# Experts' rows turned in blocks by the vector engine instead of by TensorE

## The reference, cut to what matters

```python
xn = _rmsnorm(x_flat, norm_weight, EPS)               # x * rsqrt(mean(x*x)+eps) * norm_weight
gate_vals, expert_idx = jax.lax.top_k(probs, TOP_K)
dispatch = jnp.zeros((E, CAP, Hd), x.dtype).at[e_flat, slot].add(contrib)
dm = dispatch[MLP_START:]                             # 12 experts x 1024 slots x 128 channels
h = jnp.einsum('ech,efh->ecf', dm, fc1_weight) + fc1_bias[:, None, :]
h = jax.nn.gelu(h, approximate=False)                 # 512 hidden units
out_mlp = jnp.einsum('ecf,ehf->ech', h, fc2_weight) + fc2_bias[:, None, :]
```

## Time and profile before

| | |
|---|---|
| median of 3 runs | 927.08 us |
| profiled execution | 927.48 us, of which its span is 925.7 us |
| TensorE (PE) busy | 829.0 us, 90% |
| VectorE (DVE) busy | 724.6 us, 78% |
| ScalarE (ACT) busy | 723.1 us, 78% |
| GpSimd (POOL) busy | 601.4 us, 65% |
| mean granted TensorE clock | 0.98 |

### The profile page before, as it was taken

How to read it: one execution, slowest core, us unless ns; L and a number is a source line. 1 busy time by engine, 2 the same in 40 slices (tenths; PEclk the granted TensorE clock), 3 DMA queues, 4 the chain that set the end, 5 groups by cost and what they waited for, 6 DMA issues and landing times. The chain is left out here.

```text
span 925.7 us, 20647 instructions
## 1 busy us (share of the span) xinstructions
PE 829.0 (90%) x7499; PEld 316.7 (34%) x7500; DVE 724.6 (78%) x932; ACT 723.1 (78%) x1323; POOL 601.4 (65%) x610
## 2 busy tenths in 40 slices
PE   0687269999999999999999999999999999999996
PEld 0454112222222225676867632222222222222222
DVE  5798899999999993101011089999999999999996
ACT  0578899998999897444353569899998999899996
POOL 3355247777777663999999226757567575766772
PEclk9999669999999999999999999999999999999999
DMA  8833111111111112333242211102111111210202
GB/s 221 302 68 76 32 28 33 49 40 51 51 26 40 29 45 79 112 102 121 91 142 71 94 46 22 39 20 60 37 23 45 44 36 30 70 31 17 68 17 55
DMA packets 71229, 59.39 MB, mean 64 GB/s; under 512 B 33770, under 2 KB 58178, under 8 KB 71136
## 3 DMA queue, kind: packets, MB, share of 16 engines
q1 hardware_dynamic: 61520, 48.06, 18.2%
q0 software_dynamic: 8192, 9.37, 3.9%
q10 hardware_dynamic: 1424, 0.76, 0.4%
HBM read 31.58 MB, written 30.02 MB: 67 GB/s over the span
## 5 line engine op out<-in xcount | busy, mean ns | idle before, releaser
L733 ACT ACTIVATE pr<-ps 128x512 f32<-128x512 f32 x1024 | 555.2, 595 | 57.6 <-PE ps L853 25.0
L1154 DVE TENSOR_SCALAR ps<-ps 128x1024 f32<-128x1024 f32 (+1 forms) x585 | 588.5, 1084 | 10.9 <-PE ps L843 10.9
L873 PE MATMUL ps<-pr,vp 128*32 128x256 f32 x4096 | 320.7, 391 | 3.1 <-ACT pr L733 0.2
L853 PE MATMUL ps<-q,kz 64*128 64x512 bf16 x1024 | 200.5, 389 | 25.3 <-DVE ps L1154 20.6
L843 PE MATMUL ps<-q,kz 62*128 62x512 bf16 x1024 | 196.2, 381 | 2.3 <-DMA q<-parts_dram 1.4
L519 POOL DMA_INDIRECT xs<-eout,idxs x128 | 129.0, 1008 | 95.7 <-ACT pr L733 75.7
L873 PEld LDWEIGHTS ps<-pr,vp 128*32 128x32 f32 x4096 | 86.5, 108 | 210.4 <-ACT pr L733 186.4
L504 POOL DMA_INDIRECT disp<-xn,idx x128 | 125.8, 983 | 45.8 <-ACT pr L733 26.1
L853 PEld LDWEIGHTS ps<-q,kz 64*128 64x128 bf16 x1024 | 49.0, 93 | 254.0 <-DVE ps L1154 246.3
L1174 DVE TENSOR_TENSOR pr<-ps,parts 128x1024 f32<-128x1024 f32 x12 | 14.7, 1224 | 150.8 <-PE ps L941 150.8
L759 ACT ACTIVATE pr<-ps,b1s 128x512 f32<-128x512 f32 x96 | 65.8, 687 | 53.7 <-PE ps L930 53.7
(11 more groups left out here) (122 smaller groups left out, 531.0 us busy)
## 6 DMA issues: line engine op xcount, KB each, us to landing
moved<-att SPq DMA_DIRECT2D x480, 8.0 KB
disp<-pr SPq DMA_DIRECT2D x12, 512.0 KB, 4.8
eout<-pr SPq DMA_DIRECT2D x12, 512.0 KB, 2.9
y<-in_x SPq DMA_DIRECT2D x8, 512.0 KB, 7.8
out<-y SPq DMA_DIRECT2D x7, 512.0 KB, 3.5
w<-in_w1t SPq DMA_DIRECT2D x12, 256.0 KB, 3.1
w<-in_w2t SPq DMA_DIRECT2D x12, 256.0 KB, 3.3
xs<-disp SPq DMA_DIRECT2D x6, 512.0 KB, 4.9
```

The costliest lines, as they stand in the source:

```text
L733: act.activation(pr[:, c % BUFS, 2 * pair + k, :], ps[:, score_bank(i, k), :], ACT.Exp, scale=SLOPE).then_inc(S["exps"], 1)
L853: last = pe.matmul(ps[:, score_bank(i, k), :], kz[r:r + TILE, hg, pair, kc * P:(kc + 1) * P], q2[r:r + TILE, hg, qh * HALF:(qh + 1) * HALF ...
L873: last = pe.matmul(acc[32 * g:32 * g + 32, cols], vp[:, hg, kc, g, :], pr[:, c % BUFS, g % PAIRS * 2 + g // PAIRS, cols], start=(kc == 0 a ...
L1154: last = dve.tensor_scalar(s, s, 0.0, 1.0 / SLOPE - 1.0, ALU.max, ALU.mult)
```

## The change

The loading of `dd[u]` is split into four transfers, one for each group of 32 channels. In the transfer for channels 32r to 32r+31, partition 32r + t takes, from slots t, 32 + t, 64 + t and so on, 32 channels (128 bytes) each. VectorE then turns all 32x32 blocks of the 128x1024 tile with one instruction, straight from `dd[u]` to `dt_`. TensorE's transposes and ScalarE's copies go. The norm weight is multiplied into the first weights by VectorE, in place. The first layer takes turns over six PSUM banks, 0 to 5, instead of four. Slots now lie in `dt_` in their natural order, so `store_expert` writes pieces of 512 bytes instead of 4 KB. VectorE's new `turn_rows(e + 1)` stands ahead of `expert_rows(e)` in its stream; for expert 0 it stands between the last rectification of the attention and `finish`.

```diff
@@ -183,6 +183,8 @@
         gate, rank, at, keep, tmp = (small[:, k:k + 2, :] for k in (4, 6, 8, 10, 12))
 
 
+        FB = 6
+        PER_LOAD = 16 * (4 + NR)
         hs, dt_, yo = ef[:, 0:4, :], ef[:, 4, :], ef[:, 7, :]
         dd = [xs[:].rearrange("p u t c -> p (u t c)"), ef[:, 5, :]]
         b2s = pflat[:, 0:2 * C].rearrange("p (u c) -> p u c", c=C)
@@ -203,7 +205,7 @@
                  "qz_init weighted at_rdy sum_rdy inv_rdy row_step route ones_rdy max_rdy off_rdy reset_rdy r_exp cnt_rdy pos_rdy ztile init_rdy kz_init "
                  "ld0 ld1 vp_rdy s1 relu s2 exps pv acc_evac o_rdy turned rg_rdy att_rdy spread0 spread1 y_att "
                  "scat staged pool_step carry "
-                 "ed0 ed1 etr edt fc1 gel fc2 yo_rdy yo_out gath0 gath1 comb final").split()
+                 "ed0 ed1 edt fc1 gel fc2 yo_rdy yo_out gath0 gath1 comb final").split()
         S = {n: sem(n) for n in names}
 
         block = ctx.enter_context(nc.Block())
@@ -366,14 +368,19 @@
                 for dst, src in ((w1[:, (2 * u) * FFN:(2 * u + 1) * FFN], w1t[bass.ds(e, 1), :, :].rearrange("a p f -> p (a f)")),
                                  (w1[:, (2 * u + 1) * FFN:(2 * u + 2) * FFN], w2t[bass.ds(e, 1), :, :].rearrange("a p f -> p (a f)")),
                                  (b1s[:, u, :], b1[bass.ds(e, 1), :, :].rearrange("a p f -> p (a f)")),
-                                 (b2s[:, u, :], b2[bass.ds(e, 1), :].partition_broadcast(P)),
-                                 (dd[u], disp[bass.ds(e * CAP, CAP), :].rearrange("(p j) c -> p (j c)", p=P))):
+                                 (b2s[:, u, :], b2[bass.ds(e, 1), :].partition_broadcast(P))):
                     sp.dma_start(dst, src).then_inc(S[f"ed{u}"], 16)
+
+                slots = disp[bass.ds(e * CAP, CAP), :].rearrange("(n t) c -> t n c", t=BLOCK)
+                for r in range(NR):
+                    rows = slice(BLOCK * r, BLOCK * r + BLOCK)
+                    sp.dma_start(dd[u][rows, :].rearrange("p (n c) -> p n c", c=BLOCK),
+                                 slots[:, :, rows]).then_inc(S[f"ed{u}"], 16)
 
             def store_expert(e):
                 sp.wait_ge(S["yo_rdy"], ONE + e + 1)
-                sp.dma_start(eout[bass.ds(e * CAP, CAP), :].rearrange("(p j) c -> p (j c)", p=P),
-                             yo).then_inc(S["yo_out"], 16)
+                sp.dma_start(eout[bass.ds(e * CAP, CAP), :].rearrange("(j p) c -> p j c", p=P),
+                             yo.rearrange("p (j c) -> p j c", c=C)).then_inc(S["yo_out"], 16)
 
             load_expert(0, 0)
             spread(BH * NPB - 2)
@@ -746,34 +753,25 @@
 
             attention(0, BH)
 
-            def take_turned(e):
-                for half in range(2):
-                    act.wait_ge(S["etr"], 2 * e + half + 1)
-                    act.mul(dt_[:, half * HALF:(half + 1) * HALF], ps[:, half, :], nw[:, 0:1]).then_inc(S["edt"], 1)
-
-            def expert(e, u, last):
+            def expert(e, u):
 
                 for n in range(2 * FC):
                     half, f = n // FC, n % FC
                     act.wait_ge(S["fc1"], 2 * FC * e + n + 1)
-                    act.activation(hs[:, f, half * HALF:(half + 1) * HALF], ps[:, 2 + n % 4, :], ACT.Gelu,
+                    act.activation(hs[:, f, half * HALF:(half + 1) * HALF], ps[:, n % FB, :], ACT.Gelu,
                                    bias=b1s[:, u, f:f + 1]).then_inc(S["gel"], 1)
-                if not last:
-                    take_turned(e + 1)
 
             def ready(function):
 
                 act.activation(kmax[:], gam[:], function, scale=0.0)
 
-            act.wait_ge(S["pv"], BH * NPB * TB - 1)
-            take_turned(0)
             evacuate(BH * NPB - 1)
             ready(ACT.Gelu)
             with act.Fori(0, E_MLP // 2 - 1) as k:
                 for u in range(2):
-                    expert(2 * k + u, u, False)
+                    expert(2 * k + u, u)
             for u in range(2):
-                expert(E_MLP - 2 + u, u, u == 1)
+                expert(E_MLP - 2 + u, u)
             ready(ACT.Exp)
             attention(BH, B)
             evacuate(B * NPB - 1)
@@ -901,33 +899,20 @@
                     if i > first + PAIRS and not (held and i % UP == HOLD):
                         values((i - 3) // PAIRS, (i - 3) % PAIRS)
                 values((end - 3) // PAIRS, (end - 3) % PAIRS)
-                if b1 == BH:
-                    pe.wait_ge(S["exps"], PAIRS * (end - RING + 1))
-                    turn_rows(0, 0)
                 for j in range(end - 2, end):
                     values(j // PAIRS, j % PAIRS)
 
 
-
-            def turn_rows(e, u):
-
-                pe.wait_ge(S[f"ed{u}"], 40 * (e - u) + 80)
-                wait_done(pe, "edt", 2 * e)
-                for half in range(2):
-                    for t in range(4):
-                        j = half * 4 + t
-                        last = pe.transpose(ps[:, half, t * P:(t + 1) * P], dd[u][:, j * P:(j + 1) * P], ident)
-                    last.then_inc(S["etr"], 1)
 
             def expert(e, u, first=False, last=False):
                 pe.wait_ge(S["edt"], 2 * (e + 1))
                 for n in range(2 * FC):
                     half, f = n // FC, n % FC
 
-                    pe.wait_ge(S["gel"], ONE + 2 * FC * e + max(n - 3, 0))
+                    pe.wait_ge(S["gel"], ONE + 2 * FC * e + max(n + 1 - FB, 0))
                     if n == 2 and first:
                         turn(BH * NPB - 1)
-                    pe.matmul(ps[:, 2 + n % 4, :], w1[:, 2 * u * FFN + f * P:2 * u * FFN + (f + 1) * P],
+                    pe.matmul(ps[:, n % FB, :], w1[:, 2 * u * FFN + f * P:2 * u * FFN + (f + 1) * P],
                               dt_[:, half * HALF:(half + 1) * HALF], start=True, stop=True).then_inc(S["fc1"], 1)
                 pe.wait_ge(S["turned"], NPB * BH)
                 pe.wait_ge(S["yo_rdy"], ONE + e)
@@ -941,8 +926,6 @@
                             mm = pe.matmul(o, hs[:, f, j * P:(j + 1) * P],
                                            w1[:, (2 * u + 1) * FFN + f * P:(2 * u + 1) * FFN + (f + 1) * P],
                                            start=(f == 0), stop=(f == FC - 1))
-                    if half == 0 and not last:
-                        turn_rows(e + 1, 1 - u)
                 mm.then_inc(S["fc2"], 1)
 
             ahead(0, AHEAD)
@@ -1162,7 +1145,20 @@
                     if i % UP == TURN + 1 and i > first + UP:
                         denominators(i // UP - 1)
                     rectify(i)
+                if b1 == BH:
+                    turn_rows(0, 0)
                 finish(end // UP - 1)
+
+            def turn_rows(e, u):
+
+                dve.wait_ge(S[f"ed{u}"], PER_LOAD // 2 * (e - u) + PER_LOAD)
+                weights = w1[:, (2 * u) * FFN:(2 * u + 1) * FFN]
+                dve.tensor_scalar(weights, weights, nw[:, 0:1], None, ALU.mult).then_inc(S["edt"], 1)
+                if isinstance(e, int) and e == 0:
+                    dve.wait_ge(S["pv"], BH * NPB * TB - 1)
+                else:
+                    dve.wait_ge(S["fc1"], 2 * FC * e)
+                dve.transpose(dt_, dd[u]).then_inc(S["edt"], 1)
 
             attention(0, BH)
 
@@ -1180,7 +1176,9 @@
             dve.reciprocal(gsum[:], gsum[:]).then_inc(S["inv_rdy"], 1)
             with dve.Fori(0, E_MLP // 2 - 1) as k:
                 for u in range(2):
+                    turn_rows(2 * k + u + 1, 1 - u)
                     expert_rows(2 * k + u, u)
+            turn_rows(E_MLP - 1, 1)
             expert_rows(E_MLP - 2, 0)
             for i in range(BH * NUB, BH * NUB + RING):
                 rectify(i)
```

## The result

The kernel after takes 916.78 us (915.97 to 919.07) against 927.75 (926.85 to 928.83) for the kernel before on the same chip: ratio 0.988, 95% interval 0.985 to 0.990. The time lies in the range that was given, on the side that was given, and it is the time of a rival: the forecast of 923.0 did not happen; the rival "hidden in full" had been worked out at 916.6. The profiled execution took 917.46, its span is 915.6.

The account below looks back on a forecast made before the run. TensorE's products were taken to bound the expert stretch. Period 14.02 + 0.6 = 14.6 us against 15.01 gains 4.5 over eleven experts, less 0.4 at the entry: 4.1, so median 923.0 us; range 916 to 942.

Parts of the forecast that it names:

- the forecast of 923.0: Among the experts, packets of 12 to 16 ns and a shared port: 919 to 928 us, 923.0 in the middle; chance 0.46.
- hidden in full: Load chain at or below 12.4 us, by packets of 11 ns or less or no GpSimd hold-up: 916.6 us; chance 0.20.
- What leaves: TensorE's transposes leave experts 1 to 11, 0.87 us each, period floor 14.02; ScalarE's copies and six banks worth nothing.
- VectorE's part: After the load lands, VectorE scales (0.5 us) and turns (1.23) the rows; with 0.1 for hand-overs 1.8 us.
- GpSimd's part: VectorE's scaling waits for GpSimd's instruction at a shared port pair, 1.0 us on average, from 0 to 2.35.
- The load after: From the end of a bias to the rows' landing: 6.67 + 3.5 for packets + 0.2 for the store = 10.3 us.
- 6.67 us stay: Of the earlier load's 7.92 us, 1.25 is the rows' own transfer; the other 6.67 remains in the new load.
- The sum: Chain from bias to turned rows, 13.1 us against 12.4 available; with 0.6 of lateness, period 14.6 against 15.01.
- The rival that was slower: Rows' load always late, packets above 16.5 ns, period load + 1.0 + 2.9: 928 to 959 us; chance 0.34.
- Entry and exit: Entry to the experts loses 0.4 us (-0.9 to +1.2); at the exit the last store, 0.5 us later, is covered.

## Why the prediction was right, and why its likeliest case was not

**What leaves.** Right. The floor was put at 14.02 us; it is 14.01, and giving the transposes back costs 9.9 us. Copies and banks were put at nothing and are nothing.

**VectorE's part.** Right. The turn was put at 1.23 and takes 1.23 to 1.25; the scaling at 0.5, and it takes 0.49 alone.

**GpSimd's part.** Right. The wait was put at 1.0 us on average (0 to 2.35). Nine scalings average 1.46, so the wait is 1.0. The two rows of the fence above show how it comes about: the scaling of 425.68 was issued 0.02 us after a GpSimd instruction that ran until 427.56, and it ended 0.28 behind that; the one of 439.50 began ahead of GpSimd's and took 0.49. The Trainium skill (SBUF — State Buffer, "SBUF: two separate sides") has VectorE, in some of its forms, and GpSimd block each other for a whole instruction; the trace agrees for this form, one SBUF operand and a scale, and the turn of 439.90, which took 1.24 us beside GpSimd, shows no such wait.

**The load after: the step that was mis-sized.** The prediction said 10.3 us, and it was 8.72. Its sum was "6.67 us stay", plus 3.5 for the packets, plus 0.2 for the store. The price of a packet, on which the range and the slower rival hung, was right: 13.5 ns predicted, 13.6 for the second set, and 13.6 of the engines' own time in the first. The term that was wrong is the 6.67. If the rows' packets take 3.5 of the 8.72 us, only 5.2 stay where the prediction had 6.9 with the store; that is the whole miss of 1.6. The split is not sharper than some tenths: by the broadcast's landing in the run with a quarter of the rows 5.6 stay, 1.3 below the prediction, and the packets cost the landing 3.1, 0.4 below.

It was a misreading of the earlier trace rows: the broadcast landed only 1.2 us ahead of the rows, and that was taken to mean that it ran in front of them. With other transfers behind it, it lands 1.0 us sooner. To subtract a transfer's own time from a landing is right only if the engines are busy up to that landing. In the kernel before the packets of the load and of the store ahead of it kept the engines for 5.05 of the 7.92 us to the landing; the time in which the engines stood idle between was counted as time that stays, and a part of the new packets filled it.

The Trainium skill (DMA: Bandwidth & Descriptors, "Specifications") speaks of a read-modify-write below 512 bytes. At 13.6 ns a packet of 128 bytes against 28.0 for one of 512, no surcharge shows here.

**The sum.** With 8.72 in place of 10.3 the prediction's own chain is 8.7 + 1.8 + 1.0 = 11.5 us against 12.4, 0.9 on time; the trace has about 1.0. The rival "hidden in full" asked for packets of 11 ns or less, or for no wait at the port. The wait is there, and the packets take the engines 13.6 ns: the room came from the 6.67 that was too large. So its time of 916.6 was reached for another reason than the two that it gave, and in that it was lucky. Its 0.20 was too low against the forecast's 0.46 because the whole error of the load was looked for in the packet and none in the 6.67.

**The rival that was slower.** Its formula, period = load + 1.0 + 2.9, is right on average: 16.1 against 16.15 with the rows loaded twice. Its condition was not met. The margin is small: about 1.0 us of slack on average against 3.47 for a further set of rows, so three tenths of one more set would have used it up (an estimate from these two numbers), and single experts are at the edge already.

**Entry and exit.** A loss of 0.4 was predicted (-0.9 to +1.2), and 0.6 was gained. The entry in the timeline:

```profile
344.80 0.58 SPq L372 DMA_DIRECT2D w<-in_w1t  x1
...
346.85 4.67 SPq L377 DMA_DIRECT2D xs<-disp  x4
348.86 6.96 DVE L1137 TENSOR_SCALAR ps<-ps 128x1024 f32<-128x1024 f32 x6
...
351.61 10.22 SPq L349 DMA_DIRECT2D moved<-att  x16
...
358.63 1.98 PE L915 MATMUL ps<-pr,w 128*128 128x512 f32 x4
...
361.88 0.58 SPq L372 DMA_DIRECT2D w<-in_w1t  x1
...
370.28 0.49 DVE L1156 TENSOR_SCALAR w<-w,nw 128x512 f32<-128x512 f32 x1 [8.01 <-DMA pr<-disp]
```

The start of the first load in the kernel before, and the second expert's scaling in the run of the kernel after without the broadcast:

```profile
342.98 0.58 SPq L371 DMA_DIRECT2D w<-in_w1t  x1
...
370.12 2.62 DVE L1156 TENSOR_SCALAR w<-w,nw 128x512 f32<-128x512 f32 x1 [7.92 <-DMA pr<-disp]
```

From the end of the last rectification to the first product it is 2.81 us (355.82 to 358.63) where it was 3.45. The four issues take 4.67 us ahead of the small transfers, not the 2 that 0.5 each would make; but the sixteen small transfers behind them hold SP for 10.22 us in place of 12.06. From the start of the first load to that of the second it is 17.08 us (344.80 to 361.88) against 14.90 (342.98 to 357.88), so the second load starts 2.2 later where 1.7 was predicted. It lands at 370.28, and VectorE then waits 1.56 us for TensorE ahead of the next bias. That cover is narrow: in the run without the broadcast the load landed at 370.12, the scaling met GpSimd and took 2.62 us, the bias followed without a wait, and the next one came 14.54 us later in place of 14.01. The exit costs nothing, as predicted.

## What to carry to other kernels

Work that leaves the engine which is busy without a gap is worth its full time, and its replacement elsewhere is free exactly as long as its whole chain (landing, waits at a port, operations) ends before that engine comes back; so work out the slack first, and then which term of the chain is known worst. Do not take a landing apart by subtraction: transfers that are queued one behind the other ran side by side here, and the engines stood idle for a part of the landing; read how long the packets kept the engines busy beside it. Look at the smallest slack and not only at its average. A step that costs nothing under slack (here the scaling, 1.2 us) costs its full time as soon as another term uses the slack up.

## What the runs showed that was not expected

TensorE's granted clock falls behind some of the gaps that a late load makes, and each fall is dear. In the kernel with three loads and the bias first, the sixteen products of an expert take 7.13 us at a clock of 1.00 behind a gap of 3.04 us, and 8.82 behind one of 4.67, with 0.56 of full speed (about the lower level, 1.2 GHz) in the first 2.3 us: 1.7 us lost. With the rows loaded twice it fell behind gaps of 2.06, 2.53, 3.63 and 5.22 us (0.50 to 0.62 in the first 2 us of the products, which took 8.77 to 10.07) and not behind 0.42 to 1.01 (1.00, 7.13); without the scaling not behind 1.78. The length of the gap alone does not decide: of four gaps of 3.04 us in the bias-first kernel two left the products at 7.13 us and two took them to 8.52 and 8.82. So a kernel whose load is only just late pays a little for the wait, and one whose load is later pays for the clock too, where TensorE sets the pace.

The four transfers of rows hold their issuer for longer than four single issues of 0.33 us: 3.53 us behind a store, 4.67 at the entry, 2.49 without the broadcast. With such small packets the issuing queue was a place that other issues waited at.
